# Step-size products spread between dense ones, row normalisation on ScalarE, and another order at a scan's begin, in a four-batch gated block on one core

## The chip, the cores and the metric

The kernel runs on one NeuronCore of a Trainium2 chip. Its engines are TensorE (PE in the profile, with its weight loads as PEld), VectorE (DVE), ScalarE (ACT), GpSimd (POOL) and SyncE (SP, which only issues transfers here). The metric is the device time of one execution in microseconds, lower is better.

## What is computed

Four batches of 512 rows by 512 columns pass through four residual parts. Cut to what matters:

```python
x = x + tanh(g_xattn[0]) * mamba(ctx, layernorm(x))   # 512 channels, 16 states, a scan over 512 steps
x = x + tanh(g_ffn[0]) * bitffn(layernorm(x))         # ternary weights, rows rounded to 8 bits
x = x + tanh(g_xattn[1]) * attention(layernorm(x), ctx)
x = x + tanh(g_ffn[1]) * ffn(layernorm(x))            # 512 -> 2048 -> 512, GELU

# mamba, per batch
u = silu(conv(in_proj(ctx)) + bias);  dt_low, Bm, Cm = split(x_proj(u))
dt = softplus(dt_proj(dt_low) + bias)                 # "step sizes": inner dimension 16
state = state * exp(dt * A) + (dt * u) * Bm;  y = sum_n state * Cm
```

## The kernel before

The kernel works on one batch after the other, and lays the scan of batch m = b + 1 over the last feed-forward of batch b. Each engine has its own program, written out by hand in the same order of phases; semaphores tie them together, and nothing else sets an order. The phases are:

- `opening`: projection, convolution and step sizes of batch 0, alone.
- A scan, in slots 4 to 12. It has 32 half-steps, numbered s = 2n + p for state n and half p of the channels. In each, ACT computes two decays (`decay_half`, exponentials into the PSUM pair `pairs[s % 2]`), POOL multiplies the input of a later half-step (`state_input`, four ahead), DVE runs two scans (L1430) and one product with `ccast` (L1437), and POOL adds the result to `u` by an accumulating DMA. PE spreads B and C of each state over the partitions (`scan_bcast`, always bank 0), ACT copies them to `bcast` and `ccast`, so these go one by one: product, copy, product, copy.
- During batch 0's scan (`rest=False`) PE and ACT also make the projected and convolved rows of the other three batches (`ahead`, twelve of them, at the half-steps of `AHEAD_AT`), and ACT turns the ternary weights into signs (`W_STEPS`, then `W_LATE` and `W_LAST`; each pair "scale" and "sign" is for a quarter of one matrix).
- `turning`: gate, first residual, rounding to 8 bits, start of the first feed-forward. `keep_awake(n)` issues n products of an identity that nothing reads.
- `between(b, m)`: rest of the first feed-forward of b (`up1`, `transpose_h`, `down1`), attention of b (`attend`), the normalisations, and the step sizes of m (`low_rank`, `step_sizes`, `softplus`), up to the first decays of the next scan. Row tiles i = 0 to 3 of `norm` belong to the attention, i = 4 to 7 to the last feed-forward. For these four, POOL computes 1/sigma (`norm`, `s_lnrs`), DVE normalises the row tile (`norm_apply`, L1667), PE transposes it (`norm_transpose`) and ACT copies it (`norm_copy`, L1262) into `xnT`, the operand of `f_up`, the last feed-forward's first product.
- `closing`: the last batch's feed-forwards without a scan beside them.

There are three passes with `between`, scan and `turning` (b = 0, 1, 2). In PE's `between` the four `step_sizes` products, with 16 rows of the array in use, follow each other between `transpose_h(b, 3)` and `norm_transpose(b, 2)`. `norm_transpose(b, 2)` uses bank 3 and waits until ACT has copied both halves that `transpose_h(b, 3)` left (`h_copy(b, 3)`, L1289 and L1292), and so does `down1(b, 3)`. `down1(b, 0)` of the first pass waits for all eight weight quarters (`s_wq`, 8).

## Time and profile before

| | us |
|---|---|
| median of 3 runs | 965.23 |
| lowest, highest | 961.13, 965.77 |
| the profiled execution, whole | 967.69 |
| its span in the profile | 965.9 |
| PE busy | 863.6 (89%) |
| DVE busy | 758.7 (79%) |
| ACT busy | 649.7 (67%) |
| POOL busy | 532.1 (55%) |

The busy share of an engine is an average over phases with different limits. A slice is read by asking which engine has no idle time before its instructions, and who ended the idle time of the others. Line numbers (L1667) are those of the kernel before. A float32 product of 512 columns stands in the trace as two records of some 0.43 us each at the full clock, a bf16 one as a single record of some 0.22 us from start to start; the duration printed for one record is longer, as products overlap.

### The profile page before, as it was taken

How to read it: one execution, taken by the hardware profiler on the slowest of the kernel's cores; microseconds unless marked ns; L12 is line 12 of the kernel's file. 1: busy time of each engine (PE TensorE's matmuls, PEld its weight loads, DVE VectorE, ACT ScalarE, POOL GpSimd, SP SyncE). 2: the span in 40 equal slices, each digit the busy share in tenths (PEclk: the TensorE clock that was granted, in tenths of full speed). 3: DMA queues.
4: the chain of work that ended last, by engine and by line, in shares of the span. 5: the costliest groups of instructions: out<-in, count | busy, mean ns of one | idle time of the engine just before them, and what ended most of it. 6: DMA issues, size and time to landing. Idle time of an engine off the chain costs nothing. (4 is left out here: it accounts for less than half of the span.)

```text
span 965.9 us, 9566 instructions
## 1 busy us (share of the span) xinstructions
PE 863.6 (89%) x2906; PEld 424.9 (44%) x2906; DVE 758.7 (79%) x870; ACT 649.7 (67%) x985; POOL 532.1 (55%) x461
## 2 busy tenths in 40 slices
PE   6677788689799999899799999898899999898999
PEld 2232333244344444454344444443344444447887
DVE  4698799675899999875999998956999998853333
ACT  4898898883588984654688863845689864623442
POOL 4698778121699885222898882226898871022000
PEclk9897999799899999998899999989899999998999
DMA  9189994300289985221399963401699961201231
GB/s 315 50 162 227 228 199 101 130 1 7 59 173 242 220 193 153 73 81 44 62 215 237 239 138 112 153 1 54 131 229 214 220 144 54 88 1 44 90 107 65
DMA packets 50674, 126.91 MB, mean 131 GB/s; under 512 B 6064, under 2 KB 7216, under 8 KB 50112
## 3 DMA queue, kind: packets, MB, share of 16 engines
q0 software_dynamic: 16128, 58.73, 32.9%
q1 hardware_dynamic: 34496, 67.58, 20.4%
q8 instruction: 23, 0.38, 0.2%
q14 instruction: 27, 0.22, 0.1%
HBM read 60.23 MB, written 7.34 MB: 70 GB/s over the span
## 5 line engine op out<-in xcount | busy, mean ns | idle before, releaser
L1819 POOL TENSOR_TENSOR work<-du,bcast 128x1024 f32<-128x1024 f32 x128 | 344.7, 2707 | 15.4 <-ACT bcast L986 15.1
L1430 DVE TENSOR_TENSOR_SCAN pair<-pair,work 128x512 f32<-128x512 f32 x256 | 299.2, 1215 | 26.0 <-ACT pair L1001 25.9
L1001 ACT ACTIVATE pair<-dt,a_neg 128x512 f32<-128x512 f32 x256 | 166.0, 684 | 33.1 <-DVE work L1437 32.8
L767 PE MATMUL bank<-stage,ring 128*128 128x512 f32 x384 | 178.0, 607 | 1.2 <-ACT stage L1262 1.2
L1437 DVE TENSOR_TENSOR work<-pair,ccast 128x1024 f32<-128x1024 f32 x128 | 156.8, 1225 | 12.2 <-DVE pair L1430 0.9
L1834 POOL DMA_DIRECT2D u<-work x112 | 112.6, 1005 | 54.1 <-DVE work L1437 36.3
L767 PEld LDWEIGHTS bank<-stage,ring 128*128 128x128 f32 x384 | 74.2, 195 | 85.4 <-issue 77.9
L1805 POOL TENSOR_SCALAR fst<-fst 128x1 f32<-128x1 f32 x32 | 11.3, 353 | 151.3 <-DVE fst L1659 151.1
L781 PE MATMUL bank<-ring,stage 128*128 128x512 f32 x192 | 85.6, 594 | 1.7 <-ACT hx L1297 1.7
L512 PE MATMUL bank<-xd,pick 128*128 128x512 bf16 x128 | 49.6, 387 | 25.7 <-ACT bcast L986 20.1
L649 PE MATMUL pair<-w1q,qT 128*128 128x512 bf16 x256 | 62.5, 396 | 9.6 <-ACT qT L1240 6.9
L703 PE MATMUL pair<-w2q,hx 128*128 128x512 bf16 x256 | 63.9, 407 | 1.8 <-issue 1.8
L566 PE MATMUL bank<-hx,ring 128*128 128x512 f32 x96 | 50.4, 674 | 14.7 <-ACT hx L1032 14.7
L986 ACT ACTIVATE bcast<-bank 128x512 f32<-128x512 f32 x64 | 37.4, 585 | 36.0 <-PE bank L512 35.2
L754 PE MATMUL pair<-attT,stage 128*128 128x512 f32 x128 | 57.7, 595 | 0.2 <-ACT stage L1262 0.2
L781 PEld LDWEIGHTS bank<-ring,stage 128*128 128x128 f32 x192 | 36.0, 190 | 46.5 <-issue 42.6
L986 ACT ACTIVATE ccast<-bank 128x512 f32<-128x512 f32 x64 | 37.6, 587 | 16.0 <-PE bank L512 16.0
L781 PE MATMUL bank<-ring,hx 128*128 128x512 f32 x96 | 43.5, 595 | 2.3 <-DVE stage L1713 2.3
L512 PEld LDWEIGHTS bank<-xd,pick 128*128 128x128 bf16 x128 | 12.6, 99 | 70.4 <-ACT bcast L986 34.5
L781 PE MATMUL bank<-ring,hT 128*128 128x512 f32 x96 | 42.7, 592 | 0.0
L649 PEld LDWEIGHTS pair<-w1q,qT 128*128 128x128 bf16 x256 | 24.4, 101 | 39.8 <-ACT qT L1240 8.4
L1267 ACT ACTIVATE ccast<-ccast,expo,mst 128x512 f32<-128x512 f32 x16 | 12.4, 809 | 42.9 <-DVE mst L1638 42.9
(179 smaller groups left out, 1514.3 us busy)
## 6 DMA issues: line engine op xcount, KB each, us to landing
u<-work POOLq DMA_DIRECT2D x112, 512.0 KB, 5.8
ring<-ffn_dram SPq DMA_DIRECT2D x120, 256.0 KB, 4.9
ring<-ffn_dram SPq DMA_DIRECT2D x16, 512.0 KB, 3.3
xres<-x_dram SPq DMA_DIRECT2D x4, 1024.0 KB, 5.4
stage<-w_dram SPq DMA_DIRECT2D x1, 4096.0 KB, 16.9
stage<-w_dram SPq DMA_DIRECT2D x4, 1024.0 KB, 8.0
out_dram<-stage SPq DMA_DIRECT2D x16, 256.0 KB, 2.2
ahead_dram<-hT SPq DMA_DIRECT2D x12, 256.0 KB, 3.2
```

The lines of the kernel that those rows point to most:

```text
L512: pe.matmul(banks[0][:], pick[:, i * NS + n:i * NS + n + 1].broadcast_to([P, P]), xd3[:], start=True, stop=True).then_inc(s_bc, 1)
L649: last = pe.matmul(banks[4 + g % 3][:], qT[:, k, t * P:(t + 1) * P], w1q[:, k, c * 512:(c + 1) * 512], start=k == 0, stop=k == J - 1)
L703: last = pe.matmul(banks[7][:], hqT[:, f, :], w2q[:, f, :], start=f == 0, stop=f == FT - 1)
L754: last = pe.matmul(banks[ATT_BANKS[t]][:], xnT[:, k, t * P:(t + 1) * P], attT[:, k, :], start=k == 0, stop=k == J - 1)
L767: last = pe.matmul(banks[UP_BANKS[f % 3]][:], piece(b, f)[:, k * P:(k + 1) * P], xnT[:, k, :], start=k == 0, stop=k == J - 1)
L781: last = pe.matmul(banks[2 + t % 2][:], h_tile(block)[:, t * P:(t + 1) * P], piece(b, k), start=f == 0, stop=f == FT - 1)
L986: act.activation(dst[:, n % 2, :], banks[0][:], ACT.Copy).then_inc(s_bcc, 1)
L1001: act.activation(pairs[s % DECAYBUFS][:, q, :], dt[:, p * HALF + q, :], ACT.Exp, scale=a_neg[:, p * HALF + q, n:n + 1]).then_inc(s_decay, 1)
L1430: dve.tensor_tensor_scan(pair[:, q, :], pair[:, q, :], rows[:, q, :], 0.0, ALU.mult, ALU.add).then_inc(s_scan, 1)
L1437: dve.tensor_tensor(rows, pair[:], ccast[:, n % 2, :].unsqueeze(1).broadcast_to([P, HALF, L]), ALU.mult).then_inc(s_hc, HALF)
L1819: pool.tensor_tensor(work[:, s % SCANBUFS, :, :], du[:, p * HALF:(p + 1) * HALF, :], bcast[:, n % 2, :].unsqueeze(1).broadcast_to([P, HALF ...
L1834: pool.dma_start(u[:, js, :], work[:, s % SCANBUFS, :, :], accum_op=ALU.add).then_inc(s_acc[p], 16)
```

## The change

What it does, by place:

- `AHEAD_AT`: the twelve rows made ahead stand at half-steps 3, 5, ... 25 instead of three groups 3 to 9, 12 to 18 and 21 to 27.
- `opening`: 20 of 22 fillers between the step sizes and the first broadcasts go; ACT copies the first broadcast before `rates`, and scales `u` (`skip_input`) behind the first decays.
- The end of batch 0's scan: the wait for the last row made ahead and 16 fillers in slot 12 go. `first_turning` has that wait, 24 fillers ahead of the gate's transposes (40 before) and 28 behind them.
- Weights: four steps (two quarters) ahead of `turning` instead of six, two behind it, and the last two in `between(0)`, ahead of the SiLU of `u`.
- `step_sizes` and `softplus` in `between` take a list of tiles; the products stand one by one between others.
- `norm_apply` of i = 4 to 7 moves from DVE to ACT, as scale and bias. POOL computes the bias (-mean/sigma, one more operation of 128x1) before it raises `s_lnrs`; in `closing` DVE still normalises.
- The scan's begin: on ACT, decay 0, normalise 6, decay 1, copy of the first `ccast`, normalise 7. PE makes that broadcast after transposing row tile 5. The second query/key product moves from slot 4 to slot 5.

```diff
-W_LATE = (("scale", 1, 0), ("sign", 1, 0), ("scale", 1, 1), ("sign", 1, 1), ("scale", 1, 2), ("sign", 1, 2))
+W_LATE = (("scale", 1, 0), ("sign", 1, 0), ("scale", 1, 1), ("sign", 1, 1))
+W_LATER = (("scale", 1, 2), ("sign", 1, 2))
-AHEAD_AT = {3 + 9 * g + 2 * j: J * g + j for g in range(len(AHEAD_BATCHES)) for j in range(J)}
+AHEAD_AT = {3 + 2 * a: a for a in range(AHEADS)}
...
             def first_turning(m):
+                pe.wait_ge(s_aout, AHEADS)
                 keep_awake(24)
-                keep_awake(16)
                 pe.wait_ge(s_wq, 4)
                 gate_transposes(m, (0, 1, 2, 3))
+                keep_awake(28)
...
                 step_sizes(m, None)
-                keep_awake(10)
+                keep_awake(2)
                 scan_bcast(m, 0, 0)
-                keep_awake(12)
                 scan_bcast(m, 1, 0)
...
-                    if not rest and slot == SLOTS - 1:
-                        pe.wait_ge(s_aout, AHEADS)
-                        keep_awake(16)
...
-                    if slot == QK_SLOT:
+                    if slot == (QK_SLOT + 1 if rest else QK_SLOT):
                         qk_products(m, prev, 1)
-                        if rest:
-                            norm_transpose(b, 6)
-                            norm_transpose(b, 7)
+                    if slot == QK_SLOT and rest:
+                        norm_transpose(b, 6)
+                        norm_transpose(b, 7)
...
+            def norm_apply(b, i):
+                t = i % T
+                act.wait_ge(s_lnrs, ln_count(b, i))
+                if i >= T + 2:
+                    act.wait_ge(s_xnT, b * 2 * T + i - 1)
+                act.activation(xn[:, i % 2, :], xb[:, t, :], ACT.Identity, scale=fst[:, t, 17:18],
+                               bias=fst[:, t, 19:20]).then_inc(s_xn, 1)
...
-                    rsqrt(pool_f, b, st[:, 8:9], st[:, 7:8], LN_EPS, st[:, 9:10], s_lnrs)
+                    rsqrt(pool_f, b, st[:, 8:9], st[:, 7:8], LN_EPS, st[:, 9:10])
+                    carry_wait(pool, "pool")
+                    pool.tensor_scalar(fst[:, i % T, 19:20], st[:, 6:7], st[:, 9:10], -1.0, ALU.mult,
+                                       ALU.mult).then_inc(s_lnrs, 1)
```

What stands in a row on PE in `between` of the first pass, before: L718 is `transpose_h`, L754 `attend`, L739 `norm_transpose`, L703 `down1`, L596 `step_sizes`.

```order
L718 MATMUL bank<-identb,hx 128x128 x16
L754 MATMUL pair<-attT,stage 128x512 x4
L739 MATMUL bank<-ident,stage 128x128 x4
L703 MATMUL pair<-w2q,hx 128x512 x16
L718 MATMUL bank<-identb,hx 128x128 x16
L596 MATMUL bank<-xd,dtw 128x512 x2
L596 MATMUL pair<-xd,dtw 128x512 x2
L739 MATMUL bank<-ident,stage 128x128 x4
L703 MATMUL pair<-w2q,hx 128x512 x16
```

And in the changed kernel, whose lines are a few further on (L721, L757, L742, L706, L598):

```order
L721 MATMUL bank<-identb,hx 128x128 x16
L598 MATMUL bank<-xd,dtw 128x512
L757 MATMUL pair<-attT,stage 128x512 x4
L598 MATMUL bank<-xd,dtw 128x512
L742 MATMUL bank<-ident,stage 128x128 x4
L706 MATMUL pair<-w2q,hx 128x512 x16
L598 MATMUL pair<-xd,dtw 128x512
L721 MATMUL bank<-identb,hx 128x128 x16
L598 MATMUL pair<-xd,dtw 128x512
L742 MATMUL bank<-ident,stage 128x128 x4
L706 MATMUL pair<-w2q,hx 128x512 x16
```

The four products of the step sizes now stand in four places, two of them around the last `transpose_h`.

On ACT at the begin of the same pass's scan, before: L986 copies a broadcast, L1001 is a decay, L1262 `norm_copy`, L1182 a copy of a query/key product.

```order
L1262 ACTIVATE stage<-bank 128x4x128
L986 ACTIVATE ccast<-bank 128x512
L1001 ACT_TABLE_LOAD
L1001 ACTIVATE pair<-dt,a_neg 128x512 x4
L986 ACTIVATE bcast<-bank 128x512
L1262 ACTIVATE stage<-bank 128x4x128
L1182 ACTIVATE xpad<-bank,bqk 128x512
L1001 ACTIVATE pair<-dt,a_neg 128x512 x2
L986 ACTIVATE ccast<-bank 128x512
L1182 ACTIVATE xpad<-bank,bqk 128x512
L1262 ACTIVATE stage<-bank 128x4x128 x2
```

In the changed kernel (L988, L1003, L1275 and L1195 are the same four, L1283 is the new `norm_apply`):

```order
L1275 ACTIVATE stage<-bank 128x4x128
L1283 ACTIVATE xn<-stage,fst 128x512
L1003 ACT_TABLE_LOAD
L1003 ACTIVATE pair<-dt,a_neg 128x512 x2
L1283 ACTIVATE xn<-stage,fst 128x512
L1003 ACTIVATE pair<-dt,a_neg 128x512 x2
L988 ACTIVATE ccast<-bank 128x512
L1283 ACTIVATE xn<-stage,fst 128x512
L988 ACTIVATE bcast<-bank 128x512
L1275 ACTIVATE stage<-bank 128x4x128
L1195 ACTIVATE xpad<-bank,bqk 128x512
L1003 ACTIVATE pair<-dt,a_neg 128x512 x2
```

Three normalisations stand between ACT's other work, the table load no longer follows the copy of the first `ccast`, and the second query/key copy is gone from this stretch.

## Rows read from the trace of the kernel before

**Rows 1.** The page, busy time, share of the span and instructions of PE

```profile
PE 863.6 (89%) x2906; PEld 424.9 (44%) x2906; DVE 758.7 (79%) x870; ACT 649.7 (67%) x985; POOL 532.1 (55%) x461
```

**Rows 2.** Busy time by stretch: PE, PEld, DVE, ACT, POOL, clock, DMA share, GB/s

```profile
264.00:387.00 123.00, 117.93 (x292) 51.59 (x293) 115.33 (x106) 94.31 (x154) 100.09 (x71) 0.99 0.85 193
```

**Rows 3.** Timeline, PE, first pass: start, us, instructions [idle before <-releaser]

```profile
256.32 3.12 PE L605 MATMUL bank<-ctxT,wqk 128*128 128x512 f32 x4 [0.67 <-ACT xpad L1182]
...
262.65 0.66 PE L739 MATMUL bank<-ident,xn 128*128 128x128 f32 x4 [2.36 <-DVE xn L1667]
...
264.00 5.30 PE L767 MATMUL bank<-stage,ring 128*128 128x512 f32 x8 [0.47 <-ACT stage L1262]
```

**Rows 4.** Timeline, DVE, the same scan's begin

```profile
229.93 0.52 DVE L1667 TENSOR_SCALAR xn<-stage,fst 128x512 f32<-128x512 f32 x1
...
249.99 0.75 DVE L1704 SCALAR_TENSOR_TENSOR stage<-pair,fst,stage 128x512 f32<-128x512 f32 x1 [1.03 <-POOL fst L1806]
...
256.54 6.05 DVE L1667 TENSOR_SCALAR xn<-stage,fst 128x512 f32<-128x512 f32 x2
262.52 2.33 DVE L1430 TENSOR_TENSOR_SCAN pair<-pair,work 128x512 f32<-128x512 f32 x2
```

**Rows 5.** Timeline, ACT, the same stretch

```profile
252.17 2.52 ACT L1001 ACTIVATE pair<-dt,a_neg 128x512 f32<-128x512 f32 x4
...
263.35 0.60 ACT L1262 ACTIVATE stage<-bank 128x512 f32<-128x512 f32 x1 [2.42 <-PE bank L739]
```

**Rows 6.** The page's groups: an ACT operation with scale and bias

```profile
L1267 ACT ACTIVATE ccast<-ccast,expo,mst 128x512 f32<-128x512 f32 x16 | 12.4, 809 | 42.9 <-DVE mst L1638 42.9
```

**Rows 7.** Timeline, POOL, the same stretch

```profile
252.66 0.55 POOL L1806 TENSOR_TENSOR fst<-fst,expo 128x1 f32<-128x1 f32 x1
...
258.46 2.63 POOL L1819 TENSOR_TENSOR work<-du,bcast 128x1024 f32<-128x1024 f32 x1
```

**Rows 8.** Timeline, PE, step sizes and the product behind, three passes

```profile
230.74 1.88 PE L596 MATMUL pair<-xd,dtw 16*128 16x512 f32 x4
...
233.04 5.30 PE L703 MATMUL pair<-w2q,hx 128*128 128x512 bf16 x16
...
430.91 3.62 PE L703 MATMUL pair<-w2q,hx 128*128 128x512 bf16 x16
...
437.17 2.85 PE L596 MATMUL pair<-xd,dtw 16*128 16x512 f32 x4
...
440.86 5.55 PE L703 MATMUL pair<-w2q,hx 128*128 128x512 bf16 x16
...
648.04 6.06 PE L703 MATMUL pair<-w2q,hx 128*128 128x512 bf16 x16
```

**Rows 9.** Timeline, ACT, second half of `h_copy(b, 3)`, first pass

```profile
229.50 1.02 ACT L1292 ACTIVATE hx<-bank 128x1024 bf16<-128x1024 bf16 x1
```

**Rows 10.** Timelines of PE, DVE and ACT in the opening

```profile
28.18 4.02 PE L582 MATMUL bank<-identb 128*128 128x512 bf16 x10
...
37.85 2.35 DVE L1430 TENSOR_TENSOR_SCAN pair<-pair,work 128x512 f32<-128x512 f32 x2 [7.62 <-ACT pair L1001]
...
41.55 1.30 ACT L1001 ACTIVATE pair<-dt,a_neg 128x512 f32<-128x512 f32 x2 [0.88 <-DVE work L1437]
```

**Rows 11.** Groups by line, DVE, 38 to 165: busy, mean ns, idle before

```profile
L1430 DVE TENSOR_TENSOR_SCAN pair<-pair,work 128x512 f32<-128x512 f32 x64 | 74.9, 1215 | 16.2 <-ACT pair L1001 16.2
```

**Rows 12.** Timelines of PE and ACT in the first turning

```profile
164.72 8.79 PE L582 MATMUL bank<-identb 128*128 128x512 bf16 x40
...
184.18 5.88 PE L649 MATMUL pair<-w1q,qT 128*128 128x512 bf16 x16 [0.69 <-ACT qT L1240]
...
196.35 2.08 ACT L1401 ACTIVATE stage<-stage,expo,wstat 128x2048 f32<-128x2048 f32 x1
...
200.38 2.48 ACT L1250 ACTIVATE stage<-pair,mst 128x512 f32<-128x512 f32 x4
```

**Rows 13.** Timeline, DVE, first gate tile behind the second scan

```profile
387.48 0.75 DVE L1619 SCALAR_TENSOR_TENSOR xres<-bank,gates,xres 128x512 f32<-128x512 f32 x1 [2.78 <-PE bank L625]
```

More of the change, by code:

```diff
@@ L589, in low_rank, with step_sizes @@
                 last.then_inc(s_xdbl, 1)
-            def step_sizes(b, prev):
-                pe.wait_ge(s_xd, b + 1)
-                if prev is not None:
-                    pe.wait_ge(s_gelu, prev * T * FC + T * FC)
-                for j in range(J):
+            def step_sizes(b, prev, js=range(J)):
+                if 0 in js:
+                    pe.wait_ge(s_xd, b + 1)
+                    if prev is not None:
+                        pe.wait_ge(s_gelu, prev * T * FC + T * FC)
+                for j in js:
                     pe.matmul(banks[DT_BANKS[j]][:], dtw[:, j * P:(j + 1) * P], xd[0:R, :],
@@ L859, in between @@
                 transpose_h(b, 2)
+                step_sizes(m, b, (0,))
                 attend(b, 0)
+                step_sizes(m, b, (1,))
                 norm_transpose(b, 1)
                 down1(b, 2)
+                step_sizes(m, b, (2,))
                 transpose_h(b, 3)
-                step_sizes(m, b)
+                step_sizes(m, b, (3,))
                 norm_transpose(b, 2)
@@ L873, in between @@
                 attend(b, 3)
+                norm_transpose(b, 5)
                 scan_bcast(m, 0, 1)
-                norm_transpose(b, 5)
             def closing(b):
@@ L1013, in decays @@
                     if n == 0 and part == 0 and prev is not None:
+                        norm_apply(prev, 6)
                         act.wait_ge(s_x3, prev * T + T)
@@ L1016, in decays @@
                         decay_half(b, 2 * n + 1 + part)
+                    if n == 0 and part == 0:
+                        if prev is None:
+                            skip_input(b)
+                        else:
+                            first_copy(b, prev, 0, 1)
+                            norm_apply(prev, 7)
             def project_copy(b, j):
@@ L1065, in low_rank_copy, with softplus @@
                 act.activation(xd3[:], banks[0][:], ACT.Copy).then_inc(s_xd, 1)
-            def softplus(b, prev):
+            def softplus(b, prev, js=range(J)):
                 if prev is not None:
                     act.wait_ge(s_y, prev * 2 + 2)
-                for j in range(J):
+                for j in js:
                     act.wait_ge(s_dtmm, b * J + j + 1)
@@ L1139, in between @@
                 gelu1(b, 3)
+                if b == 0:
+                    for step in W_LAST:
+                        weight(*step)
                 silu_u(m)
@@ L1145, in between @@
                 norm_copy(b, 1)
+                softplus(m, b, (0, 1, 2))
                 h_copy(b, 3)
-                softplus(m, b)
+                softplus(m, b, (3,))
                 norm_copy(b, 2)
+                norm_apply(b, 4)
                 first_copy(m, b, 0, 0)
@@ L1153, in between @@
                 norm_copy(b, 4)
-                first_copy(m, b, 0, 1)
+                norm_apply(b, 5)
             def closing(b):
@@ L1331, in pass_ @@
                         ahead(slot, 0, 1)
-                    if slot == QK_SLOT:
+                    if slot == (QK_SLOT + 1 if rest else QK_SLOT):
                         qk_copy(m, prev, 1)
-                        if rest:
-                            norm_copy(b, 6)
-                            norm_copy(b, 7)
+                    if slot == QK_SLOT and rest:
+                        norm_copy(b, 6)
+                        norm_copy(b, 7)
                     if rest:
@@ L1361, in pass_ @@
                 if not rest:
-                    for step in W_LAST:
+                    for step in W_LATER:
                         weight(*step)
@@ L1510, in between @@
                 second(b, 2)
-                norm_apply(b, 4)
                 step_inputs(m, 0)
@@ L1515, in between @@
                 third(b, 1)
-                norm_apply(b, 5)
                 third(b, 2)
@@ L1747, in pass_ @@
                     half(m, prev, slot, 0, 0)
-                    if rest and slot == 4:
-                        norm_apply(b, 6)
-                        norm_apply(b, 7)
                     half(m, prev, slot, 0, 1)
```

5 lines of the change are left out of this document (2 added, 3 removed).

## The prediction

> **What bounds the kernel now.** I read the page's busy times first: PE is busy 863.6 of 965.9 us [rows 1], so it comes first in every phase. Then the busy time by stretch: in a scan of a pass PE is busy 117.93 of 123 us and DVE 115.33 [rows 2], so both are nearly full. The end of that scan decides between them. DVE is through with the gate and idles 2.78 us until PE's transposes come [rows 13]; a group of four transposes takes some 0.6 us of it, so PE is about 2 us behind. Hence PE sets a pass, and a gain counts only if PE's last feed-forward starts earlier.
>
> The begin of a scan, by timelines, shows where PE stands still. The attention's last residual starts on DVE at 249.99 [rows 4], which I take as the pass's mark A. PE starts `f_up` at 264.00, 14.0 us later, after waiting 2.36 us for DVE's normalised row tile [rows 3]. The two `norm_apply` in front of it take 6.05 us, though one alone took 0.52 [rows 4]; POOL's product at 258.46 lies inside the second [rows 7]. Both engines want the same data path, and DVE's next scans stand behind, at 262.52.
>
> The last thing read is the stretch after the step sizes [rows 8]. Sixteen bf16 products of `down1` take 3.62 us at the full clock, and 5.30, 5.55 and 6.06 behind the step sizes. PE was never idle there; it ran sixteen-row products.
>
> The sum is made against the profiled execution, 967.7 us, which is 2.5 above the median of 965.2; the prediction is given against the median.
>
> **1. A scan's begin, three passes.** DVE loses 6.05 us of normalising [rows 4]; ACT gets four operations per pass at 0.81 us, the price of a like one with scale and bias [rows 6]. In time from A, after: ACT has decay 0 done by 0.5, since it no longer waits for the copy of `ccast`. Row tile 6 follows, then decay 1, which must wait for the residual to be read (0.75), to 2.3, and the copy to 2.9. POOL ends the seventh tile's 1/sigma at 3.2 (252.66 plus 0.55) [rows 7] and needs some 0.4 for the extra operation, so ACT normalises tile 7 at 3.6 to 4.4. Behind it in ACT's queue stand a broadcast copy, `norm_copy(5)`, the query/key copy (1.9 together), then decay 2, which waits for DVE's first half-step at about 5.9 and ends near 7.3, a broadcast copy, and `norm_copy` 6 and 7 at 0.5 to 0.6 each [rows 5]. `f_up` starts near 9.2 instead of 14.0: 4.8 earlier. The second query/key product then stands in the feed-forward's stream instead of in idle time: four records of 0.43, 1.7 us. Net 3.1 us on PE. DVE's second half-step comes at 5.9 instead of 12.5, 6.6 earlier, so the pauses that PE makes for DVE and ACT in the scan (123 less 117.93, 5.1) shrink; I take 1.1 of them. So **4.2 per pass, 12.6 in all**. Ends: 3.1 per pass (9.3) if none shrink, 6.6 (19.8) if PE follows DVE wholly.
>
> **2. Step sizes, three passes.** What the low clock costs [rows 8]: 5.30 less 3.62 is 1.7; in the second pass 5.55 less 3.62, plus 2.85 less 1.88, is 2.9; in the third 6.06 less 3.62 is 2.4. Together 7.0. Against it: the products covered ACT's copy of `transpose_h(b, 3)`, which ends at 230.52 [rows 9], 1.6 us after the transposes, and now ends some 0.3 later since softplus of the third tile stands before it. `norm_transpose(b, 2)` waits for it behind one product of 0.86 instead of four: PE idles 1.05 per pass, 3.15 in all. And that stretch (a product, sixteen transposes, a product, the wait, four transposes) still holds no dense product for 4 us, so the clock may fall there; then half of `down1` runs low, 1.7 per pass as in the first pass now. Never: gain 3.85. Always: loss 1.25. I take two of three, **gain 0.45**.
>
> The Trainium skill speaks here ("TensorE: Matmul & The Clock Gate", Part 4: PE-mode transpose): transposes do not count as busy the way products do. By that rule the low clock is likely in all three passes, and this term is its loss end; rows 8 only show that sixteen-row products do not hold the clock.
>
> **3. Opening and first scan.** Ten fillers take 4.02 us [rows 10] and twelve more follow the first broadcast. With two left, the first broadcast comes near 29 instead of 32, and ACT's chain behind it (copy, rates, two copies, decay) puts the first scan at 34.7 instead of 37.85. ACT soon takes most of it back: its next decays waited only 0.88 for DVE [rows 10], and from there ACT is full; it carries 1.3. Inside the scan DVE idles 16.2 less the first 7.62, 8.6 us, always for a decay [rows 11]. In the old table the second group of rows made ahead falls on the same half-steps (p = 0) as most weight steps, ACT's longest pieces; the new one puts all on p = 1. I take half of the 8.6, **5.5 together**. Ends: 1.3 and 11.7.
>
> **4. First turning and weights.** PE runs 40 fillers to 173.4 [rows 12] while DVE's gate was done at 170.6, and ACT has six weight steps ahead of its rounding. A pair holds ACT for 4.03 us (196.35 to 200.38) [rows 12]; two steps fewer let everything start 4 us earlier. The same 4 us come back in `between(0)`, where `down1(b, 0)` waits for the last quarter. What stays: 28 fillers before `up1` should hold the clock, so that its 16 products take about 3.6 instead of 5.88 [rows 12], 2.2; PE then idles in front of `down1`, which starts at the low clock, 1.7 lost; ACT's small waits, 0.7. **Gain 1.2**, ends -1.9 (fillers in the way of ready transposes, clock low at both) and 3.3.
>
> **5. Closing.** POOL's extra operation is bare in front of the last tile: **loss 0.5**, no more.
>
> Sum: 12.6 + 0.45 + 5.5 + 1.2 - 0.5 = 19.25. 965.2 - 19.2 = **946.0** (948.4 for the profiled execution).
>
> **Rivals.**
> - *DVE sets the scan, not PE.* For it: DVE is busy 115 of 123. Then term 1 is 19.8 and the sum 26.4: 938.8; with term 3 near its end, 932. Against it: rows 13. Chance 0.13.
> - *Small gain.* Term 1 stays at 9.3, the clock falls every pass as the skill's rule has it (term 2 at -1.25), and ACT gives the opening back (term 3 at 2.5): with terms 4 and 5 the sum is 11.2, 954.0. For it: nothing in the rows shows that ACT's full first scan yields. Chance 0.2.
> - *Slower.* One mechanism: `norm_copy` 6 and 7 stand behind decay 2 on ACT, which waits for DVE's first half-step, and tile 7 behind POOL's 1/sigma. If ACT's chain slips, `f_up` starts no earlier, while the query/key product (1.7) and the bare copy (1.05) now cost PE 8.3 in three passes. With terms 3 to 5 (6.2 gained) a slowdown of 4.8 needs `f_up` more than 14.9 behind A; at 16 it is 973. Against it: my chain has 5 us to spare. Chance 0.04.
> - *It does not do what it says*: first scan unchanged and `f_up` near 12.5, where gain and cost cancel: 963 to 966. Chance 0.04.
>
> The forecast's own case, 939 to 952, has 0.59. The range takes in the small gain and part of the DVE case: 936 to 956. Half a per cent (4.8 us) is what a measurement of this kernel can tell from no change. Faster by more than that: 0.91; same 0.05; slower 0.04.
>
> **What would show it.** In the changed profile: `f_up` (L770) 8.5 to 10 us behind the last attention residual, and a DVE without L1667 in the scans; ACT's L1283 at 0.6 to 0.8 us each; sixteen `down1` products behind the last step size at 3.6 (clock held) or 5.3 (fallen); the first scan near 34.7, the last of batch 0 ending near 159; gate transposes still awaited by DVE after each scan. The forecast is wrong if PE's idle time in the scans grows by what `f_up` gained, if DVE waits for decays longer than now, or if PE stands still for more than 2 us in front of `down1(b, 3)`.

## The result, and the profile after

The changed kernel takes **950.97 us** (median of 4 runs, 950.64 to 952.13) where the kernel before took 963.18 in the same comparison (960.51 to 965.77): ratio 0.9876, 95% interval 0.984 to 0.9911. That is 12.2 us of gain. The forecast was 946.0 and 19.25 us of gain, with a range of 936 to 956 that holds the measured time. The sign and the main term were right, and some 7 us of the sum did not arrive. The profiled execution took 950.86 us, its span 949.0.

The page, busy times, beside [rows 1]: VectorE gave 27 us away and ScalarE took 10.

```profile
PE 849.1 (89%) x2842; PEld 418.9 (44%) x2882; DVE 732.0 (77%) x858; ACT 659.2 (69%) x997; POOL 539.0 (57%) x477
```

The scan's begin in the first pass, timelines (start, us, engine and line, operation, count, idle time before and its releaser). First VectorE, to be held against [rows 4]:

```profile
249.48 0.75 DVE L1723 SCALAR_TENSOR_TENSOR stage<-pair,fst,stage 128x512 f32<-128x512 f32 x1 [2.28 <-PE pair L757]
...
251.56 2.35 DVE L1451 TENSOR_TENSOR_SCAN pair<-pair,work 128x512 f32<-128x512 f32 x2 [0.28 <-ACT pair L1003]
...
255.14 2.33 DVE L1451 TENSOR_TENSOR_SCAN pair<-pair,work 128x512 f32<-128x512 f32 x2
```

then ScalarE, with the two row tiles that it now normalises (L1283):

```profile
250.00 0.80 ACT L1283 ACTIVATE xn<-stage,fst 128x512 f32<-128x512 f32 x1
...
252.81 0.81 ACT L1283 ACTIVATE xn<-stage,fst 128x512 f32<-128x512 f32 x1 [0.31 <-POOL fst L1891]
```

and TensorE, beside [rows 3]:

```profile
252.56 0.61 PE L513 MATMUL bank<-xd,pick 128*128 128x512 bf16 x1 [2.47 <-ACT ccast L988]
252.96 3.28 PE L607 MATMUL bank<-ctxT,wqk 128*128 128x512 f32 x4
...
258.73 0.39 PE L513 MATMUL bank<-xd,pick 128*128 128x512 bf16 x1 [1.40 <-ACT ccast L988]
259.70 3.70 PE L770 MATMUL bank<-stage,ring 128*128 128x512 f32 x8 [0.58 <-ACT stage L1275]
```

`f_up` starts 10.2 us behind mark A (the attention's last residual, here 249.48) instead of 14.0, and VectorE's second half-step comes 5.7 us behind A instead of 12.5. The products before `f_up` run at the lower clock (3.28 us where four take 1.88 at the full one). In the second and third pass it is otherwise: `f_up` starts 8.65 us behind A, and its own first eight products run low, in some 5.4 us where they take 3.70 at the full clock. The second pass, A at 451.35:

```profile
460.00 5.40 PE L770 MATMUL bank<-stage,ring 128*128 128x512 f32 x8 [0.58 <-ACT stage L1275]
```

TensorE's granted clock has two levels, 2.4 GHz (granted 1.00) and 1.2 GHz (0.50); "the clock fell" means from the first to the second. The busy times of a stretch at the lower level, 460.58 to 463.99, inside those eight products (columns as in [rows 2]):

```profile
460.58:463.99 3.41, 3.41 (x6) 1.34 (x5) 3.32 (x4) 1.66 (x4) 3.41 (x3) 0.50 0.82 156
```

Behind the scan VectorE still waits for the gate's transposes for the same 2.78 us as in [rows 13], and the scan's stretch is as full on TensorE as in [rows 2] (columns as there):

```profile
382.45 0.75 DVE L1638 SCALAR_TENSOR_TENSOR xres<-bank,gates,xres 128x512 f32<-128x512 f32 x1 [2.78 <-PE bank L627]
```

```profile
259.70:382.00 122.30, 117.87 (x292) 51.74 (x297) 112.46 (x104) 95.20 (x155) 102.30 (x73) 1.00 0.88 196
```

So TensorE is still the later of the two. The third thing to read is the way from the first scan to the first `down1` of batch 0. VectorE's first scan, and its group of scans from 35 to 162 (beside [rows 10, 11]); then ScalarE and TensorE behind the scan (beside [rows 12]):

```profile
35.28 2.35 DVE L1451 TENSOR_TENSOR_SCAN pair<-pair,work 128x512 f32<-128x512 f32 x2 [4.64 <-ACT pair L1003]
```

```profile
L1451 DVE TENSOR_TENSOR_SCAN pair<-pair,work 128x512 f32<-128x512 f32 x64 | 74.9, 1216 | 13.4 <-ACT pair L1003 12.9 <-POOL work L1835 0.5
```

```profile
167.69 2.10 ACT L1422 ACTIVATE stage<-stage,expo,wstat 128x2048 f32<-128x2048 f32 x1 [4.75 <-POOL wstat L1934]
...
203.35 2.00 ACT L1428 ACTIVATE w2q<-stage,expo 128x2048 bf16<-128x2048 f32 x1
```

```profile
205.88 6.13 PE L706 MATMUL pair<-w2q,hx 128*128 128x512 bf16 x15 [4.37 <-ACT w2q L1428]
211.85 3.60 PE L589 MATMUL bank<-u,xpw 128*128 128x512 f32 x8
```

Less its first wait, VectorE waited 8.8 us inside the first scan (13.4 less 4.64), where it had waited 8.6 (16.2 less 7.62, [rows 11]): the new places of the rows ahead did not shorten these waits.

The gate's transposes came 5.7 us earlier than before (167.63 against 173.35), but A only 0.5 us (249.48 against 249.99). The last rows show where it went: TensorE stands still for 4.37 us until ScalarE has the last quarter of the second matrix, and then the products of `down1(b, 0)` take 6.1 us, where sixteen take 3.62 at the full clock.

### The profile page after: what moved, and what is told of

Same layout as the page of the kernel before. It is cut to its first block and busy times, and to the rows that moved or that the text cites. A ratio compares the mean times of both kernels' runs of the same rounds, so it can differ in the third digit from the quotient of the medians.

```text
span 949.0 us, 9513 instructions
## 1 busy us (share of the span) xinstructions
PE 849.1 (89%) x2842; PEld 418.9 (44%) x2882; DVE 732.0 (77%) x858; ACT 659.2 (69%) x997; POOL 539.0 (57%) x477
## 5 line engine op out<-in xcount | busy, mean ns | idle before, releaser
L1003 ACT ACTIVATE pair<-dt,a_neg 128x512 f32<-128x512 f32 x256 | 166.1, 685 | 21.6 <-DVE work L1458 21.4
L1821 POOL TENSOR_SCALAR fst<-fst 128x1 f32<-128x1 f32 x32 | 13.5, 421 | 146.8 <-DVE fst L1678 146.8
L651 PE MATMUL pair<-w1q,qT 128*128 128x512 bf16 x247 | 58.7, 383 | 11.4 <-ACT qT L1253 7.8
L513 PE MATMUL bank<-xd,pick 128*128 128x512 bf16 x108 | 42.6, 395 | 25.3 <-ACT ccast L988 14.3
L706 PE MATMUL pair<-w2q,hx 128*128 128x512 bf16 x245 | 58.9, 392 | 6.7 <-ACT w2q L1428 4.4
L757 PE MATMUL pair<-attT,stage 128*128 128x512 f32 x128 | 57.9, 596 | 0.3 <-ACT stage L1275 0.3
L988 ACT ACTIVATE bcast<-bank 128x512 f32<-128x512 f32 x64 | 37.7, 588 | 21.4 <-PE bank L513 20.1
L988 ACT ACTIVATE ccast<-bank 128x512 f32<-128x512 f32 x64 | 37.7, 589 | 11.8 <-PE bank L513 11.0
L706 PEld LDWEIGHTS pair<-w2q,hx 128*128 128x128 bf16 x256 | 25.5, 100 | 35.1 <-issue 8.0
```

What stands on the lines that cost most here:

```text
L651: last = pe.matmul(banks[4 + g % 3][:], qT[:, k, t * P:(t + 1) * P], w1q[:, k, c * 512:(c + 1) * 512], start=k == 0, stop=k == J - 1)
L706: last = pe.matmul(banks[7][:], hqT[:, f, :], w2q[:, f, :], start=f == 0, stop=f == FT - 1)
L757: last = pe.matmul(banks[ATT_BANKS[t]][:], xnT[:, k, t * P:(t + 1) * P], attT[:, k, :], start=k == 0, stop=k == J - 1)
L988: act.activation(dst[:, n % 2, :], banks[0][:], ACT.Copy).then_inc(s_bcc, 1)
L1003: act.activation(pairs[s % DECAYBUFS][:, q, :], dt[:, p * HALF + q, :], ACT.Exp, scale=a_neg[:, p * HALF + q, n:n + 1]).then_inc(s_decay, 1)
```

## The experiments

The twelve experiments were compared with the kernel before, four at a time on one chip. The runs of one kernel (5 to 12) lie within 1 to 10 us of one another; in the profiles the clock falls in some passes and not in others. So parts of 1 to 3 us are read in the traces, one profiled execution of each kernel, by times worked out from the timelines: the first scan's end; the start of the second group of sixteen `down1` products of batch 0 (G, 216.21 in the kernel before, 215.72 in the changed one); from the second group to A in each pass; from A to the gate's transposes in each pass. The last two hardly vary but for the clock. The first two vary by several us from one profile to another (160.25 to 165.68 and 211.92 to 217.87 in three kernels with the old opening), so differences of their means are weaker evidence.

### The base again

No edit (a_again).

> The changed kernel once more, as the base that the three kernels beside it are read against. Expected: 951 us, 0.988 of the kernel before (the result was 950.97, 0.984 to 0.991).

Measured: 952.45 us, ratio 0.9855 (0.9827 to 0.9883), runs from 949.7 to 955.42; before 963.88. The gain is there in a second comparison, 11.4 us. In its third pass the clock fell behind the step sizes, though they are spread:

```profile
634.42 1.12 PE L598 MATMUL pair<-xd,dtw 16*128 16x512 f32 x2
636.76 5.19 PE L706 MATMUL pair<-w2q,hx 128*128 128x512 bf16 x16
```

### The scan's begin undone

```diff
-                        norm_apply(prev, 6)
...
-                            first_copy(b, prev, 0, 1)
-                            norm_apply(prev, 7)
...
-                norm_apply(b, 4)
...
-                norm_apply(b, 5)
+                first_copy(m, b, 0, 1)
...
-                    if slot == (QK_SLOT + 1 if rest else QK_SLOT):
+                    if slot == QK_SLOT:
                         qk_products(m, prev, 1)
```

Run u_begin, cut to its main lines. The first are ScalarE's, which give the four normalisations back to VectorE; the last are TensorE's. GpSimd's extra operation goes too.

> The changed kernel with the scan's begin of before: the two normalisations on DVE, the broadcast and copy order and the second query/key product where they were. Theory A (the step counted for 12.85 us in the trace pair, 4.5, 4.0 and 4.3 from the attention's last residual to the gate transposes): 963.8 us, f_up again 13 to 14 us behind the residual instead of 10.2. Rival B (it is the whole of the measured 12.2 and the other edits come to nothing together, -0.6): 963.2. Rival C (part of the gain belongs to other edits, such as the clock at the scan's begin, which the trace pair can't divide): 958 to 961. This is the term that I am surest of.

Measured: 964.19 us, ratio 0.9993 (0.997 to 1.0017). Without this edit nothing is left of the gain: it is worth 11.7 us by the medians (964.19 less 952.45). The trace shows the old picture, with the two normalisations at 6.06 us again and `f_up` 14.4 us behind A (249.60):

```profile
256.15 6.06 DVE L1683 TENSOR_SCALAR xn<-stage,fst 128x512 f32<-128x512 f32 x2
```

```profile
264.00 2.44 PE L770 MATMUL bank<-stage,ring 128*128 128x512 f32 x3 [0.26 <-ACT stage L1270]
```

From A to the gate's transposes: 136.85, 136.47 and 136.75 us in the kernel before, 136.87, 136.51 and 136.77 here, 132.33, 132.46 and 132.41 in the changed kernel: 4.3 per pass. The edit is a bundle: the engine that normalises, ScalarE's order around the decays, the place of the first broadcast's copy, and the place of the second query/key product. Only the last was also tried alone (b_qk); how the rest divides isn't shown.

### The step sizes in one row again

Run u_steps; ScalarE's `softplus` becomes one call again too.

```diff
                 transpose_h(b, 2)
-                step_sizes(m, b, (0,))
                 attend(b, 0)
-                step_sizes(m, b, (1,))
                 norm_transpose(b, 1)
                 down1(b, 2)
-                step_sizes(m, b, (2,))
                 transpose_h(b, 3)
-                step_sizes(m, b, (3,))
+                step_sizes(m, b)
```

> The changed kernel with the four step size products in one row again, and ACT's softplus likewise: the spread alone is undone. The sixteen products of down1 behind the last step size should again take 5.3 to 6.1 us where they take 3.62 in the changed kernel's profile. Theory A (the trace pair's reading: the clock is held in all three passes, and the stretch from the gate transposes to the attention's last residual is 1.7 us shorter in two passes and 0.24 in the first): 3.6 us slower than the changed kernel, 954.6. The prediction's term: 0.45, 951.4. Rival B (the medians' reading: the profiled execution of before lay 4.5 us above its median, so the pair overstates; the copy in front of norm_transpose costs what the clock gives): 0 to 1.5 us faster than the changed kernel, 949.5 to 951.

Measured: 949.30 us, ratio 0.9823 (0.9798 to 0.9848), 3.1 below the base beside it (3.2 by the means of six runs each, with a standard error of 1.3). Theory A is false, and rival B has the right sign. The row of eight, first pass, clock held, and second pass, clock fallen:

```profile
225.60 1.98 PE L598 MATMUL bank<-xd,dtw 16*128 16x512 f32 x4
227.42 1.87 PE L598 MATMUL pair<-xd,dtw 16*128 16x512 f32 x4
...
229.72 3.62 PE L706 MATMUL pair<-w2q,hx 128*128 128x512 bf16 x16
```

```profile
427.67 2.48 PE L598 MATMUL pair<-xd,dtw 16*128 16x512 f32 x4
...
430.99 5.92 PE L706 MATMUL pair<-w2q,hx 128*128 128x512 bf16 x16
```

The row doesn't always let the clock fall. From the second `down1` group to A a pass takes 32.10 us with the row and a held clock, 33.76 with the spread and a held clock, and 33.7 to 35.5 with a fall, in either form. The spread's own price, 1.66, is the wait for ScalarE's copy (0.65) and some 1.0 of changes between kinds of products, as TensorE has no other wait in either stretch:

```profile
231.98 1.12 PE L598 MATMUL pair<-xd,dtw 16*128 16x512 f32 x2
233.75 0.63 PE L742 MATMUL bank<-ident,stage 128*128 128x128 f32 x4 [0.65 <-ACT hx L1313]
234.21 3.62 PE L706 MATMUL pair<-w2q,hx 128*128 128x512 bf16 x15
```

(changed kernel, first pass; one record of the sixteen is missing). Two step products take 1.05 us from start to start of what follows when alone, 0.91 inside the row.

### Only the parts within the passes

Run o_scan, cut to its main lines.

```diff
-W_LATE = (("scale", 1, 0), ("sign", 1, 0), ("scale", 1, 1), ("sign", 1, 1))
+W_LATE = (("scale", 1, 0), ("sign", 1, 0), ("scale", 1, 1), ("sign", 1, 1), ("scale", 1, 2), ("sign", 1, 2))
-AHEAD_AT = {3 + 2 * a: a for a in range(AHEADS)}
+AHEAD_AT = {3 + 9 * g + 2 * j: J * g + j for g in range(len(AHEAD_BATCHES)) for j in range(J)}
...
-                keep_awake(2)
+                keep_awake(10)
                 scan_bcast(m, 0, 0)
+                keep_awake(12)
...
-                keep_awake(28)
```

> Only the parts within the passes are kept (the scan's begin and the spread of the step sizes); the opening's fillers and ACT order, the rows made ahead, the fillers of the first turning and the place of the weight steps are those of the kernel before. Theory A (what the opening, the first scan and the first turning gained, 5.7 us up to the gate transposes, was given back in front of down1(b, 0), where 0.5 us is left): 951.5 us. Rival B (the forecast's terms 3 and 4, 6.7 us, are there and something else in the passes lost them): 957.7. Rival C (they cost time net): below 950.5.

Measured: 951.10 us, ratio 0.9847 (0.9821 to 0.9874). That is theory A's number: everything outside the passes comes to nothing together, within the scatter of the runs (948.79 to 954.77). It also showed how far one kernel's first scan can vary. Its code up to 160 us is that of the kernel before, it starts at 37.88 (37.85 there), and ends at 160.25 instead of 164.67. By stretch, the kernel before first, this one second (columns as in [rows 2]):

```profile
90.00:145.00 55.00, 45.29 (x99) 18.36 (x99) 46.77 (x44) 46.91 (x71) 40.57 (x27) 0.88 0.94 219
```

```profile
90.00:145.00 55.00, 44.94 (x107) 18.33 (x108) 50.21 (x48) 50.57 (x77) 43.51 (x29) 0.97 1.00 233
```

The granted clock is 0.88 in one and 0.97 in the other, and TensorE, busy for the same 45 us, has eight products fewer in the first. VectorE, ScalarE and GpSimd get less done in it as well. So the same code can differ by 4.4 us in the first scan, and the slower one has the lower clock; the 16.2 us of waits in [rows 11] were not all due to the places of ScalarE's work. That the clock is the cause and not a companion wasn't tried.

### The begin alone

Run only_begin: the kernel of the last experiment with the step sizes in one row too, which is the kernel before plus the new begin.

> The kernel before with the changed begin of the scan alone: no spread, and opening, rows ahead, first turning and weights as before. Theory A (what the runs so far say part by part: the spread costs 1.66 us of TensorE's time per pass at either clock, from the start of the second group of down1 products to the start of the fourth, 18.49 against 16.83 in the profiles with and without it, and saves a fall of the clock in one pass of three at about 2.2 us; the other parts bring nothing): 3 us faster than the begin with the spread (951.1), so 948. Rival B (the spread is neutral, and 949.3 without it was chance): 951 to 952. Rival C (the parts need one another): over 953.

Measured: 948.25 us, ratio 0.985 (0.9805 to 0.9896), runs from 945.48 to 955.26. The median is theory A's number, but runs this wide apart don't tell it from rival B. Against the kernel before (964.0 in this comparison) the begin alone brings 15.7 us, more than the whole change. From the other side than the experiment that undoes it, this too says that the begin is where the gain lies.

### Rows ahead at their old places

Run u_ahead.

```diff
-AHEAD_AT = {3 + 2 * a: a for a in range(AHEADS)}
+AHEAD_AT = {3 + 9 * g + 2 * j: J * g + j for g in range(len(AHEAD_BATCHES)) for j in range(J)}
```

> The changed kernel with the old places of the rows made ahead in the first scan. Theory A (the first scan is full on ScalarE, and the new places bring nothing): 952.4 as the changed kernel, plus or minus 1. The prediction's term (half of the 8.6 us in which VectorE waits for a decay): 4.2 slower, 956.6. Rival C (the new places cost: the scan lasts 126.3 to 127.5 us from first to last in four profiles with them and 122.4 in one with the old places): 2 to 4 faster, 949 to 950, with the last scan of batch 0 ending near 158 instead of 161.5.

Measured: 948.98 us, ratio 0.9855 (0.9817 to 0.9893). Its first scan ends at 159.30, as rival C has it, but the other profiles widen that: with the shorter opening and the old places it ends at 159.30, 160.89, 162.40, 162.53 and 163.00 (mean 161.6), with the new places at 161.37 to 161.62 in all six (mean 161.5). So at the scan's end the new places bring nothing on average, and the prediction's 4 us for them were not there. Behind the scan they cost: ScalarE's first weight step starts at 167.69 to 168.13 with them and at 165.25 to 166.69 without, and G is 213.24 here, 2.5 us earlier than in the changed kernel (1.1 earlier than in its repeat, 214.33) with the same low clock in front of it. That is rival C by another road. With the old opening the first scan ends at 160.25, 164.67 and 165.68 (mean 163.5): the opening is worth 1.9 there, with a standard error of 1.8.

Why the new places end the scan so evenly isn't settled, but the granted clock differs. From the first scan to the last it is 0.84 to 0.86 in the six profiles with the new places and 0.89 to 0.94 in the eight with the old ones. The changed kernel, and o_scan, whose first scan is the shortest of all (columns as in [rows 2]):

```profile
35.28:161.60 126.32, 97.98 (x224) 40.46 (x228) 114.02 (x103) 117.30 (x188) 104.68 (x76) 0.86 0.83 183
```

```profile
37.88:160.25 122.37, 90.26 (x224) 36.25 (x223) 113.73 (x103) 110.97 (x178) 105.30 (x76) 0.94 0.85 189
```

In these profiles TensorE is longer at the full clock with the twelve rows in three groups than with them spread out. Whether that lower clock took back what the places gave wasn't tried.

### The second matrix by quarters

Run w_quarters.

```diff
-                else:
-                    pe.wait_ge(s_wq, 8)
                 for f in range(FT):
+                    if b == 0 and t == 0 and f % 4 == 0:
+                        pe.wait_ge(s_wq, 5 + f // 4)
```

> The changed kernel in which the first group of down1 products asks for the second matrix a quarter at a time (four products, then the next quarter) instead of for the whole of it. Theory A (this wait, 4.37 us, and the low clock behind it, 6.1 instead of 3.6 us, gave back the gain of the opening; twelve products then lie in the wait and hold the clock): the products end by 206.5 instead of 211.8, low_rank waits for silu_u, which ends at 208.6, and the attention's last residual comes 3 us earlier: 949.4. Rival B (something else is next, such as ScalarE's copies of the low rank product, and takes the 3 us back before the scan): under 1 us, 951.5 to 952.4.

Measured: 951.69 us, ratio 0.9861 (0.9823 to 0.9899); rival B's number, by a mechanism that neither named.

```profile
201.66 2.75 PE L706 MATMUL pair<-w2q,hx 128*128 128x512 bf16 x12
205.73 1.04 PE L706 MATMUL pair<-w2q,hx 128*128 128x512 bf16 x4 [1.31 <-ACT w2q L1428]
208.95 6.46 PE L589 MATMUL bank<-u,xpw 128*128 128x512 f32 x8 [2.18 <-ACT u L1063]
```

The products are done by 206.8 instead of 212, as theory A says. Then `low_rank` waits 2.18 us for silu, and its eight products take 6.46 us instead of 3.60. G is 215.69, 215.72 in the changed kernel: the low clock only moved to what stands behind the last pause.

### The weight steps in their old order

Run u_weights.

```diff
-W_LATE = (("scale", 1, 0), ("sign", 1, 0), ("scale", 1, 1), ("sign", 1, 1))
+W_LATE = (("scale", 1, 0), ("sign", 1, 0), ("scale", 1, 1), ("sign", 1, 1), ("scale", 1, 2), ("sign", 1, 2))
...
-                    for step in W_LATER:
+                    for step in W_LAST:
...
-                if b == 0:
-                    for step in W_LAST:
-                        weight(*step)
                 silu_u(m)
```

> The changed kernel with six weight steps in front of the first turning again and only the last two behind its first part. Theory A (only ScalarE's total matters up to down1(b, 0), which then waits for up1's products instead of for the weights): within 1 us of 952.4, up1 of batch 0 starting 3 to 4 us later. The prediction's term counted 4 us at the start that come back as a wait and 1.2 net: 953.6. Rival C (without the wait in front of down1 the clock holds there): 2.5 us faster, 950.

Measured: 950.39 us, ratio 0.9852 (0.9814 to 0.989).

```profile
206.26 3.62 PE L706 MATMUL pair<-w2q,hx 128*128 128x512 bf16 x16
209.72 3.60 PE L589 MATMUL bank<-u,xpw 128*128 128x512 f32 x8
```

`down1(b, 0)` starts 0.4 us later than in the changed kernel and at the full clock, so G is 213.59 instead of 215.72. That is rival C's mechanism, 2.1 us where it put 2.5; the median shows it within its noise, since later passes of this profile fell. Over all profiles: with the new order the first stretch behind the wait ran at the low clock in five of six (`down1` at 6.1 to 6.5 us, or `low_rank` as above), with the old order in none of eight (3.62).

### Without the three edits that cost

Run b_plain: the changed kernel with the step sizes in one row, the old places of the rows ahead and the old order of the weight steps; the diffs are those above.

> The changed kernel without the three edits that the runs so far show as costs: step size products in one row, old places of the rows made ahead, old order of the weight steps. The new scan's begin, the shorter opening and the new fillers of the first turning stay. Theory A (the costs add up: 5.0 us for the spread in three passes less some 2 us of clock regained, 2.3 us for the rows ahead by the length of the first scan, 2.1 us for the weight order by the start of the second down1 group): 7.4 below the changed kernel's 952.4, 945. Rival B (the first scan and the first turning take back whatever is gained in front of them, by the low clock): as the begin alone, 948.3.

Measured: 946.10 us, ratio 0.9812 (0.9781 to 0.9844), runs from 944.96 to 947.2. That is 1.1 above theory A's number, and all five runs are below rival B's. It is compared with the changed kernel across two comparisons, in which the kernel before had 963.38 and 963.88. G is 211.07 us, and 211.20 to 211.67 in the three kernels below, which share this part; 213.59 with the new places of the rows ahead (u_weights), 215.7 with the new order too. So the two edits cost some 2.3 and 2.1 us there. Part of the first cost is seen on GpSimd, whose four small operations stand between the scan and the first weight step. The first three of them in the changed kernel, and here:

```profile
163.11 1.10 POOL L1926 TENSOR_SCALAR wstat<-wstat 128x1 f32<-128x1 f32 x1
164.30 1.38 POOL L1927 TENSOR_TENSOR wstat<-wstat,expo 128x1 f32<-128x1 f32 x1
165.75 1.04 POOL L1928 TENSOR_TENSOR wstat<-wstat,expo 128x1 f32<-128x1 f32 x1
```

```profile
162.32 0.24 POOL L1919 TENSOR_SCALAR wstat<-wstat 128x1 f32<-128x1 f32 x1
162.65 0.56 POOL L1920 TENSOR_TENSOR wstat<-wstat,expo 128x1 f32<-128x1 f32 x1
163.28 0.55 POOL L1921 TENSOR_TENSOR wstat<-wstat,expo 128x1 f32<-128x1 f32 x1
```

The fourth takes 0.61 there and 1.96 here, so the four last 4.6 us and 3.7; they also start 0.8 later there. By the timelines, the slow ones (the fourth here, from 164.08, too) lie beside VectorE's operations on two SBUF tensors behind the scan (from 162.84 in the changed kernel, from 163.65 here), and the quick ones beside the scan's last operations, which read PSUM. That these operations are what slows them wasn't tried.

### The step sizes in two groups

Run b_half, shown against b_plain.

```diff
                 transpose_h(b, 2)
+                step_sizes(m, b, (0, 1))
                 attend(b, 0)
...
                 transpose_h(b, 3)
-                step_sizes(m, b)
+                step_sizes(m, b, (2, 3))
@@ ScalarE @@
+                softplus(m, b, (0, 1))
                 h_copy(b, 3)
-                softplus(m, b)
+                softplus(m, b, (2, 3))
```

> As the kernel beside it (b_plain), with the step sizes in two groups: two behind transpose_h(b, 2) and two behind transpose_h(b, 3), which cover ScalarE's copy. Theory A (the spread's 1.66 us per pass are 0.65 of TensorE waiting for that copy and 1.0 of changing between kinds of products six times; with one change more instead of three, and the copy mostly covered, 0.4 per pass is left, and no row of eight is there to let the clock fall): 0.5 to 2.5 faster than b_plain, 943.5, sixteen down1 products at 3.62 in every pass. Rival B (the clock falls as often as with one row, and the groups only add their cost): 1.2 us slower, 946.

Measured: **942.84 us**, ratio 0.9781 (0.9749 to 0.9813), 3.3 below b_plain (3.1 by the means, standard error 0.6): theory A, and more. It has the lowest median of the study, with b_fill only 0.6 above.

```profile
226.44 1.98 PE L598 MATMUL pair<-xd,dtw 16*128 16x512 f32 x4
228.34 0.66 PE L742 MATMUL bank<-ident,stage 128*128 128x128 f32 x4
228.84 3.62 PE L706 MATMUL pair<-w2q,hx 128*128 128x512 bf16 x16
```

No wait stands in front of the transposes, and the second group to A takes 32.43 us in all three passes, 0.34 more than one row with the clock held (32.09) and without its falls (33.78 and 35.42 in two passes of b_plain). One profile was taken, so "no fall" stands on three passes.

### Fillers in the pause at the scan's begin

Run b_fill, shown against b_plain.

```diff
                 for slot in range(4, SLOTS):
+                    if rest and slot == 4:
+                        keep_awake(9, 1)
                     bcast_next(m, slot, 0, 0)
```

> As b_plain, with nine fillers of 512 columns in the 2.47 us in which TensorE waits for a broadcast's copy in front of the first query/key product. Theory A (that pause and the 1.40 us behind it let the clock fall, so that the query/key product takes 3.3 instead of 1.9 us or the first eight feed-forward products 5.2 instead of 3.7, in one pass of two): 1 to 2.5 us faster than b_plain. Rival B (the clock falls anyway, later, and the fillers at the low clock outlast the pause by 1.3 us): 0 to 2 us slower.

Measured: 943.44 us, ratio 0.9784 (0.9753 to 0.9815), runs from 943.1 to 943.89; 2.7 below b_plain: theory A. Without the fillers, and with them:

```profile
247.93 0.60 PE L513 MATMUL bank<-xd,pick 128*128 128x512 bf16 x1 [2.47 <-ACT ccast L985]
248.32 3.41 PE L607 MATMUL bank<-ctxT,wqk 128*128 128x512 f32 x4
```

```profile
245.57 2.11 PE L583 MATMUL bank<-identb 128*128 128x512 bf16 x9
248.20 0.39 PE L513 MATMUL bank<-xd,pick 128*128 128x512 bf16 x1 [0.53 <-ACT ccast L987]
248.43 1.88 PE L607 MATMUL bank<-ctxT,wqk 128*128 128x512 f32 x4
```

`f_up` starts 8.65 us behind A in all three passes (10.34, 9.43 and 10.19 without), and A to the gate's transposes takes 130.76 us in two of three. In the first pass the clock fell behind the next pause instead, and it is 132.46. This kernel and b_half put together were not run.

### The second query/key product back in slot 4

Run b_qk, shown against b_plain, TensorE's lines.

```diff
-                    if slot == (QK_SLOT + 1 if rest else QK_SLOT):
+                    if slot == QK_SLOT:
                         qk_products(m, prev, 1)
```

> As b_plain, with the second query/key product back in the fourth slot, in front of the last two row tiles' transposes. The prediction counted 1.7 us per pass that this product costs in the feed-forward's stream, since it had stood in idle time. Theory A (in slot 4 it waits for ScalarE's copy of the first one, and row tiles 6 and 7 stand behind it: f_up starts 1.5 to 2 us later and the gain is nil): within 1 us of b_plain. Rival B (the prediction's 1.7 is real and regained): 3 to 5 us faster. Rival C (f_up is later by more than the product's time): 2 to 5 slower.

Measured: 944.76 us, ratio 0.9796 (0.9766 to 0.9825), 1.3 below b_plain with runs that overlap.

```profile
252.59 1.98 PE L607 MATMUL bank<-ctxT,wqk 128*128 128x512 f32 x4 [0.56 <-ACT xpad L1188]
...
256.33 3.70 PE L770 MATMUL bank<-stage,ring 128*128 128x512 f32 x8 [0.66 <-ACT stage L1268]
```

`f_up` starts 11.4 us behind A, 1.0 to 2.0 later, and A to the gate takes 131.8 in each pass, 132.1 on average in b_plain: theory A, no difference beyond 0.3 per pass. The two parts are larger. From `f_up` to the gate's transposes it is 120.39 us here and 122.10 in b_plain, in all three passes of each, so the product does take the 1.7 us in the feed-forward's stream. It is not regained, because in slot 4 it holds up `f_up` by 1.0 us or more.

## Why the prediction was right, and where its sum was not

- **Term 1, the scan's begin** (12.6 forecast). Right in mechanism and size: 4.3 us per pass from A to the gate's transposes, 12.9 in all, and 11.7 by the medians with the edit undone. The pieces, worked out from the three passes before and after: `f_up` came 10.22, 8.65 and 8.65 us behind A, 9.2 on average as forecast, and 5.0 earlier where 4.8 was forecast. The query/key product costs 1.7 as charged (b_qk). Of the 1.1 put down to shorter pauses, 0.5 was there; another 0.6 was the clock, which the sum did not hold, so that part of the match is luck. The first eight products of `f_up` ran low in all three passes before ([rows 3]: 5.30 us, not read by the prediction as a fall) and in two of three after, at 1.7 a time. In the remaining pass the fall stood in front of `f_up` and made it the 10.22. ScalarE's normalisation took 0.80 and 0.81, as read from [rows 6]. That TensorE sets the scan and not VectorE holds: the gate is awaited for 2.78 us as before, and VectorE's second half-step came 6.9 to 7.2 us earlier while the pass became only 4.3 shorter, so the rival with VectorE as the bound fell.
- **Term 2, the spread** (0.45 gained forecast). Measured a loss. The second `down1` group to A takes 34.31 us on average over 21 passes of seven profiles with the spread and 33.94 over 18 passes of six with the row: 0.36 per pass, **1.1 lost** in three. The standard error of the 0.36 is 0.37, so the traces alone don't tell the loss from nothing; the medians, 3.1 apart with and without the spread, put it higher. The failed step is "what the low clock costs": the prediction took the profiled execution's three falls in [rows 8] as what a row of eight always does. It fell in 13 of 18 passes, so that the falls cost 5.6 us per execution on average and not 7.0. With the spread it fell in 7 of 21; the guess of two passes in three was too dark (1.6 us instead of 3.4). But the bare price was 1.66 us per pass, 5.0 in three, and not 1.05 and 3.15, because besides the wait (0.65) every change to and from these products costs, and that was not in the sum. The Trainium skill's rule that the prediction weighed ("TensorE: Matmul & The Clock Gate", Part 4: PE-mode transpose: transposes don't count as busy) made a fall likely in every pass. The traces don't agree: 14 of 21 passes held the clock through that stretch.
- **Term 3, opening and first scan** (5.5 forecast). Measured **2.0** at the first scan's end, by the means above (standard error 1.7), and all of it the opening's. The first scan started at 35.28, near the 34.7 forecast, and ended at 161.60, not 159. The step that failed is "I take half of the 8.6": nothing in the rows said that VectorE's waits for decays belong to where the rows ahead stand. With the new places they are 8.8 us, no shorter, and o_scan shows the same code 4.4 us faster in an execution with a higher clock (0.94 against 0.91 over the scan).
- **Term 4, first turning and weights** (1.2 gained forecast). **1.4 lost.** G is 215.3 on average in the three profiles with the old opening and turning (211.92, 216.21, 217.87) and 214.7 in the four with all of the new (212.89, 214.33, 215.72, 215.84): 0.6 for terms 3 and 4 together, with a standard error of 1.9, so that the 1.4 is a difference of two weak means. Firmer are the parts, from kernels that share more: opening and fillers alone bring 4.0 (211.3, mean of four); the new places take 2.3 back behind the scan; the new order takes 1.1 on average, 2.1 where the clock falls. The wait in front of `down1` and the low clock behind it were named, but priced at 1.7 for half of the products, and all of them ran low, 2.5. That the new places push the first weight step back by 2 us was in no step of the sum.
- **Term 5, closing** (0.5 lost forecast): from the last gate transposes to the last residual 63.87 us before and 64.52 after, 0.65.

The sum of what was found is 12.9 - 1.1 + 0.6 - 0.65 = 11.75, and 12.2 and 11.4 were measured; with the standard errors above, the closeness is partly luck. All of the missing 7 to 8 us lie in terms 2 to 4, and terms 2 and 3 had the same fault: one profiled execution was read as the rule for things that vary with the clock from one execution to the next. That execution, 967.69 us, itself lies 3.8 above the median of 17 runs (963.88). Of the signs that the prediction named, the `f_up` times, the 0.8 us of ScalarE's L1283, the 3.62 of `down1` and the first scan near 34.7 came; the end of batch 0's scan near 159 did not. The small-gain rival (954.0) had named ScalarE's full first scan and the loss by the spread, with the scan's begin too low.

## What to carry to other kernels

The whole gain came at one place, where 6 us of normalising on VectorE held up TensorE: it went to ScalarE, which had slack, and ScalarE's order was fitted to it. It could be sized to 3% from the rows around one mark, with the clock's part by luck. A pause of TensorE costs twice, itself and the products behind it at the lower clock, and taking the wait away only helps if the next pause doesn't inherit the low clock: fill the pause, or order the work so that none is left. Where small-row products have to be spread, put them into the places where they cover a wait, in groups, not one by one (b_half). And take the price of a fall of the clock from several profiles, not from one.

## What the runs showed of the hardware

- A row of eight sixteen-row products keeps TensorE without idle time, and still the clock fell in or behind it in 13 of 18 passes of six programs; in the others it held. Within one program it also differs from pass to pass (b_plain: 4.92, 6.04 and 3.62 us for the sixteen products behind). Eleven executions of the kernel before on one chip lie between 959.2 and 968.3 us.
- Changing from dense products to two sixteen-row ones and back cost 0.14 us and more over the same two inside a row (1.05 against 0.91 from start to start).
- A fall of the clock at the begin of the last feed-forward costs 1.7 us: eight products in 5.40 us instead of 3.70. From A to the gate's transposes a pass takes 130.76 us without a fall, some 132.4 with one, and 134.04 with two (b_fill, the changed kernel, u_weights).
- GpSimd's operations on a single column took 1.10, 1.38 and 1.04 us beside one mix of VectorE work and 0.24, 0.56 and 0.55 beside another, right behind the same scan.
